# A graph layer on one Trainium2 core: 51 dense blocks and 1520 gathered tiles in place of 52 and 1480

## The chip, the core and the metric

One NeuronCore of a Trainium2 chip. TensorE is written PE (PEld is its weight load), VectorE DVE, ScalarE ACT, GpSimd POOL, SyncE SP. The metric is the device time of one execution in microseconds; lower is better.

## The reference

There are 12500 nodes with 128 features each and 400000 edges, sorted by destination. `src` and `dst` are the two ends of each edge.

```
h = relu(layernorm(x))
att = sigmoid(h[src] @ W_att[:128] + h[dst] @ W_att[128:] + b_att)
messages = (h[src] @ W_msg + b_msg) * att
aggregated = segment_sum(messages, dst)
r, z, n = the gates of a GRU cell with input aggregated and state h
h_new = (1 - z) * n + z * h
out = x + batch norm of h_new over the nodes (gamma, beta)
```

## The kernel before

**Two ways for an edge.** A node has 32 incoming edges on average. The destinations are cut in two: the first D0 = 12500 - 128 * BLOCKS = 5844 nodes are "gathered", the last 52 blocks of 128 nodes are "dense". Both ways read a table with one row per node: 128 message features, the source's score, and (in SBUF only) the destination's score.

A *gathered tile* is 128 consecutive edges. POOL issues one indirect DMA for it (line 782), which brings the 128 rows of the sources from HBM into a ring of ten buffers, `row_ring`. ACT makes the sigmoid of the scores (`gate`, line 906), DVE multiplies it by a mask of destinations (`mask`, line 1193), and PE adds rows times mask into a window of 64 nodes (`scatter`, line 1450, two matmul instructions). Ten tiles are a group; DVE adds each group's window to the sums (`add_group`, line 1201). SPARSE = 1480 tiles cover the first 189440 edges. Four groups are a set of 40 tiles, whose indices SP loads two sets deep.

A *dense block* gathers nothing. Its 64 pairs of destinations have at most 128 edges each. DVE makes one-hot matrices of the sources' low and high parts (`lo_hots`, line 1172, and `key_hots`, line 1179, eight of each in a block), PE multiplies them into a count of edges from every source to every destination (`build`, line 1460), ACT makes the sigmoid for all 98 x 128 sources against the block's destinations (`dense_gate`, line 910, 98 instructions), DVE multiplies counts and gates (`keep_pairs`, line 1209, sixteen), and PE multiplies the result with the whole message table (`block_part`, line 1465, 98 steps of two matmul instructions in 36 parts).

**The order.** It is written out by hand: 53 units of 40 steps, the same loops on every engine. In unit u PE and DVE build block u, ACT makes the gates of block u + 1 from step 7 on (`dense_at`), and PE multiplies block u - 1 from step 3 on. `first_tile` and `tiles_before` spread the gathered tiles over all steps of the first 52 units, 28 or 29 to a unit (14 units have 29), the last ten being left for unit 52. The GRU jobs, one for each dense block and one for each 128 gathered nodes (52 + 46 = 98 jobs), have fixed steps too (`gru_jobs`). On an engine all instructions of a step are issued in program order, so a late tile holds back the dense work behind it, and the reverse. In a step PE issues the tile's scatter before anything else.

**What a gather waits for.** POOL does nothing but gathers between the search at the start and the end. Gather t waits until the tile of ten places before has been multiplied (`tiles_summed`), and for its set of indices; then it is issued.

```
for t in range(SPARSE):
    if t % SET == 0:
        set_ready(pool, t // SET)
    wait_reuse(pool, tiles_summed, t + 1 - ROWS_RING)
    nc.gpsimd.indirect_dma_start(row_ring[:, t % ROWS_RING, :], None, table, ...)
```

`lo_hots` and `key_hots` are DVE operations with both inputs in SBUF and bf16 output; `keep_pairs` reads one input from PSUM.

**Before and behind the units.** At the start the table is made from x in 25 chunks, while the first edge of each pair of dense destinations is found by a search: `find_tiles` compares the queries D0, D0 + 2, ... with the first destination of every row of tiles (`row_first`) and with that of the next row (`row_next`, set at line 748). There are 26 columns of 128 queries. At the end come batch norm and the output in 25 chunks.

If any of several assumptions on the edges fails (a group wider than its window, a pair with over 128 edges, gathered tiles that don't reach D0), a count is not zero, and a slow path recomputes everything (`if_slow`).

Of the kernel before, what the change touches and what calls it, by code (L numbers as in the profile page):

```python
# [16 lines left out]
TPC = CHUNK // P  # L17
EPS = 1e-5

BLOCKS = 52  # L20
UNITS = BLOCKS + 1
STEPS_U = 40
SET = 40
GROUP = 10
GROUPS_S = SET // GROUP
SPARSE = 1480
SETS = SPARSE // SET
GROUPS = SPARSE // GROUP
LAST_TILES = 10
WIN = 64  # L30
PAIR = 2
# [22 lines left out]
def first_tile(u):  # L54

    return (SPARSE - LAST_TILES) * u // BLOCKS if u <= BLOCKS else SPARSE


def tiles_before(u, s):

    n = first_tile(u + 1) - first_tile(u)
    return first_tile(u) + (min(s, n) if u == BLOCKS else s * n // STEPS_U)

# [7 lines left out]
def groups_before(u, s):  # L71

    return GROUPS if u == BLOCKS and s > LAST_TILES + GROUP_LAG else max(0, tiles_before(u, s) - GROUP_LAG - 1) // GROUP

# [6 lines left out]
def gru_jobs(steps):  # L81

    jobs, at, gathered = [], {}, 0
    for u in range(UNITS):
        for slot, s in enumerate(GRU_AT):
            if slot in ((4,) if u == BLOCKS else (1, 3)):
                continue
            ready = sum(1 for j in range(gathered, steps) if groups_needed(j) <= groups_before(u, s))
            if slot == 0 and u >= 2:
                job = ("dense", u - 2)  # L90
            elif slot and ready >= (2 if slot == 2 and u < BLOCKS else 1):
                job = ("gather", gathered)
# [20 lines left out]
def up(n, m):  # L113
    return -(-n // m) * m
# [13 lines left out]
def gnn_program(nc, x, src, dst, W_msg, b_msg, W_att, b_att, W_ih, b_ih, W_hh, b_hh, gamma, beta, out):  # L128
    NODES, D = x.shape
# [10 lines left out]
    D0 = NODES - BLOCKS * P  # L140
# [13 lines left out]
    QTILES = QCOLS * P  # L154
# [3 lines left out]
    B_FIRST = up(D0 + P, CHUNK) // P  # L158
    assert TILES % 2 == 1 and SPARSE < TILES and FINE <= P and GROWS <= P and HI <= P and 5 * GROWS <= 512 and KEYS <= 256
    assert SPARSE % SET == 0 and GROUPS % 2 == 0 and DENSE_AT + PARTS < STEPS_U + 4 and NEW_BACK_AT > NEW_AT[0] and PARTS_AT + PARTS < STEPS_U and SETS > 2 and TILES % 16 == 5  # L160
    assert QCOLS == 2 * QHALF and (FINE + 1) * QHALF <= 512 and FINE * P <= QCOLS * P
# [5 lines left out]
    b_dram = nc.dram_tensor("dst_scores", (HI * P,), F32, kind="Internal").ap()  # L167
    idx_dram = nc.dram_tensor("sparse_src", (P, SPARSE), U32, kind="Internal").ap()
    rel_dram = nc.dram_tensor("sparse_dst", (P, SPARSE), F32, kind="Internal").ap()
# [10 lines left out]
    with ExitStack() as ctx:  # L180
# [3 lines left out]
        def sem(name):  # L184
            return ctx.enter_context(nc.semaphore(name))
# [22 lines left out]
        def place(width, rows=P):  # L208
            spot[0] += width
            return part(spot[0] - width, width, rows)  # L210
# [10 lines left out]
        row_next = place(1, COARSE)  # L221
# [123 lines left out]
        q_line_made = sem("q_line_made")  # L345
# [102 lines left out]
        def if_slow(eng, engine):  # L448

            eng.wait_ge(bad_known, 1)  # L450
            _, (total,) = nc.values_load_multi_w_load_instructions(
                bad_all[0:1, 0:1], engines=[engine], min_val=0, max_val=EDGES,
                skip_runtime_bounds_check_because="a count of windows: 0 to their number")
            register = eng.alloc_register(f"slow_{engine.name}")
            eng.reg_mov(register, total)
            return eng.If_ne(register, 0)

        def group_bases(first, n, engine):
            _, values = nc.values_load_multi_w_load_instructions(
                group_at[0:1, bass.ds(first, n)], engines=[engine], min_val=0, max_val=D0,  # L460
                skip_runtime_bounds_check_because=BOUNDED)
            return list(values)
# [267 lines left out]
        def _(pool):  # L730
# [14 lines left out]
            pool.wait_ge(ones_made, 1)  # L745
            nc.gpsimd.affine_select(out=ident, in_=ones, compare_op=ALU.is_equal, fill=0.0, base=0,
                                    pattern=[[1, P]], channel_multiplier=-1).then_inc(consts_made, 1)
            nc.gpsimd.memset(row_next, float(NODES)).then_inc(q_line_made, 1)
            nc.gpsimd.iota(starts[:, FINE:FINE + 1], [[0, 1]], base=0, channel_multiplier=FINE,
                           allow_small_or_imprecise_dtypes=True).then_inc(q_line_made, 1)  # L750
            nc.gpsimd.iota(q_line, [[PAIR, QCOLS * P]], base=D0, channel_multiplier=0,
# [821 lines left out]
```

## Time and profile before

| what | us |
|---|---|
| three runs | 2250.46, 2253.87 (median), 2258.87 |
| the profiled execution: its own time | 2247.65 |
| its span | 2245.9 |
| busy: PE, DVE, ACT, POOL | 2053.0, 2014.2, 1995.8, 1656.3 |
| first and last gather start | 145.3, 2189.1 |

The span runs from the first to the last instruction; the execution's own time has 1.75 us more around it. An engine's busy time leaves out the time its sequencer takes for issuing, waiting and semaphores. The sum of the last dense block is taken over at 2214.3 us; batch norm and the output lie behind it.

### The profile page before, as it was taken

The page shows a single profiled execution, that of the slowest core. Times are in us where ns is not written, and L with a number is a line of the kernel's source. Part 1 is how long each engine was busy: PE and PEld are TensorE (multiplying, and loading weights), DVE is VectorE, ACT ScalarE, POOL GpSimd, SP SyncE. Part 2 cuts the span into 40 slices and gives each one's busy share as a digit, 9 for nine tenths or more (in the row PEclk, how much of TensorE's full clock was granted, in tenths as well). Part 3 has the DMA queues.
Part 4 walks back from the last instruction along what each step waited for, and adds up shares of the span by engine and source line. Part 5 has one row for each costly group of instructions (what it writes and reads, how often), then busy time and mean ns, then how long its engine had stood idle before and what let it go on. Part 6 is the DMA issues. An engine that isn't in the chain of part 4 may idle for free.

```text
span 2245.9 us, 53903 instructions
## 1 busy us (share of the span) xinstructions
PE 2053.0 (91%) x18202; PEld 1989.9 (89%) x18202; DVE 2014.2 (90%) x4413; ACT 1995.8 (89%) x6980; POOL 1656.3 (74%) x1578
## 2 busy tenths in 40 slices
PE   4536999999999999999999999999999999999997
PEld 3525999999999999999999999999999999999997
DVE  5967899999999999999999999999999999999984
ACT  1368999999999999999999999999999999999944
POOL 5575777777777777777777777777777777777770
PEclk9865999999999999999999999999999999999999
DMA  7862222222222222222222222222222222222255
GB/s 175 239 163 62 56 61 61 59 61 61 61 62 63 61 60 61 62 63 58 62 61 62 60 62 60 62 61 61 62 61 62 61 61 62 62 60 63 59 163 183
DMA packets 167473, 171.57 MB, mean 76 GB/s; under 512 B 79462, under 2 KB 131736, under 8 KB 166944
## 3 DMA queue, kind: packets, MB, share of 16 engines
q0 software_dynamic: 49856, 102.96, 20.3%
q1 hardware_dynamic: 114564, 61.63, 10.9%
q10 hardware_dynamic: 2776, 3.52, 0.7%
q8 instruction: 147, 2.41, 0.4%
q14 instruction: 130, 1.06, 0.2%
HBM read 141.32 MB, written 26.65 MB: 75 GB/s over the span
## 4 chain that ended last, share of the span: by engine, by line
ACT 52%; PE 23%; DVE 16%; issue 7%; DMA 2%; DVEq 0%; POOL 0%; ACTq 0%; SPq 0%
ACT big L910 41%; PE ps L1465 12%; ACT gate_ring L906 9%; DVE big L1209 5%; PE ps L1450 4%; PE ps L1460 3%; DVE gate_ring L1193 2%; DVE key_hot L1179 1%; DVE big L1138 1%; DVE lo_hot L1172 1%; PE ps L1471 1%; PE ps L1472 1%; ACT n_blk L915 1%; DMA row_ring<-node_table,set_idx 1%; DVE big L1125 1%
## 5 line engine op out<-in xcount | busy, mean ns | idle before, releaser
L782 POOL DMA_INDIRECT row_ring<-node_table,set_idx x1480 | 1568.0, 1059 | 477.0 <-issue 329.4
L910 ACT ACTIVATE big<-set_score,big 128x128 f32<-128x128 f32 x5096 | 1630.7, 392 | 79.7 <-PE ps L1465 79.7
L1465 PE MATMUL ps<-big 128*128 128x128 f32 x10192 | 1444.4, 281 | 0.0
L1465 PEld LDWEIGHTS ps<-big 128*128 128x128 f32 x10192 | 1261.8, 192 | 0.0
L1209 DVE TENSOR_TENSOR big<-ps,big 128x784 f32<-128x784 f32 x832 | 802.0, 964 | 7.8 <-ACT big L910 5.0
L1450 PE MATMUL ps<-gate_ring,row_ring 128*128 128x64 f32 x2960 | 534.4, 263 | 75.7 <-DVE gate_ring L1193 70.5
L1450 PEld LDWEIGHTS ps<-gate_ring,row_ring 128*128 128x128 f32 x2960 | 453.3, 193 | 122.7 <-DVE gate_ring L1193 108.9
L1193 DVE SCALAR_TENSOR_TENSOR gate_ring<-lane,set_rel,gate_ring 128x64 f32<-128x64 f32 x1480 | 413.1, 280 | 136.2 <-ACT gate_ring L906 131.0
L906 ACT ACTIVATE gate_ring<-set_win,row_ring 128x64 f32<-128x64 f32 x1480 | 490.6, 339 | 27.1 <-DMA row_ring<-node_table,set_idx 23.2
L1460 PE MATMUL ps<-key_hot,lo_hot 128*128 128x196 bf16 x3328 | 425.5, 250 | 14.6 <-DVE key_hot L1179 9.9
L1179 DVE TENSOR_TENSOR key_hot<-lane_key,set_key 128x1568 bf16<-128x1568 bf16 x416 | 402.2, 967 | 0.0
L1460 PEld LDWEIGHTS ps<-key_hot,lo_hot 128*128 128x128 bf16 x3328 | 315.9, 110 | 18.7 <-issue 16.4
L1172 DVE TENSOR_TENSOR lo_hot<-lane_lo,set_lo 128x1024 bf16<-128x1024 bf16 x416 | 284.6, 684 | 6.2 <-DMA set_key<-dense_key 6.2
L1471 PE MATMUL ps<-h_blk,gates 128*128 128x128 f32 (+1 forms) x392 | 78.9, 284 | 0.5 <-DVE agg_blk L1215 0.5
L1421 PE MATMUL ps<-ident,big 128*128 128x128 f32 x98 | 20.9, 350 | 50.9 <-DVE big L1138 50.9
L1421 PEld LDWEIGHTS ps<-ident,big 128*128 128x128 f32 x98 | 13.8, 177 | 54.5 <-DVE big L1138 37.9
L1471 PEld LDWEIGHTS ps<-h_blk,gates 128*128 128x128 f32 x392 | 61.0, 196 | 0.6 <-issue 0.6
L861 ACT ACTIVATE big<-ps 128x512 f32<-128x512 f32 (+1 forms) x25 | 14.7, 587 | 52.6 <-issue 30.9
L915 ACT ACTIVATE n_blk<-ps,small 128x128 f32<-128x128 f32 (+1 forms) x98 | 34.2, 349 | 23.5 <-PE ps L1474 20.9
L767 POOL DMA_INDIRECT big<-in_dst_dram,big x26 | 26.2, 1009 | 28.3 <-DVE big L1050 20.7
L1430 PE MATMUL ps<-big 128*128 128x130 f32 x196 | 36.3, 344 | 9.9 <-ACT big L861 9.6
L1430 PEld LDWEIGHTS ps<-big 128*128 128x128 f32 x196 | 32.9, 252 | 12.3 <-ACT big L861 12.1
(129 smaller groups left out, 922.4 us busy)
## 6 DMA issues: line engine op xcount, KB each, us to landing
row_ring<-node_table,set_idx POOLq DMA_INDIRECT x1480
big<-in_x_dram SPq DMA_DIRECT2D x48, 256.0 KB, 6.6
h_blk<-hT_spill SPq DMA_DIRECT2D x97, 64.0 KB
node_table<-big SPq DMA_DIRECT2D x24, 258.0 KB
hT_spill<-big SPq DMA_DIRECT2D x24, 256.0 KB, 5.3
out_dram<-big SPq DMA_DIRECT2D x24, 256.0 KB
set_win<-dst_scores SPq DMA_DIRECT2D x148, 32.0 KB
set_score<-dst_scores SPq DMA_DIRECT2D x52, 64.0 KB, 3.0
```

Of the source, the lines that this page charges most:

```text
L782: nc.gpsimd.indirect_dma_start(row_ring[:, t % ROWS_RING, :], None, table, bass.IndirectOffsetOnAxis(ap=set_idx[:, t // SET % 2, t % SET:t ...
L906: nc.scalar.activation(gate_ring[:, t % GATES_RING, :], set_win[:, t // SET % 2, t % SET // GROUP, :], ACT.Sigmoid, bias=row_ring[:, t % R ...
L910: return nc.scalar.activation(a_buf[b % 2][:, h, :], set_score[:, b % 2, :], ACT.Sigmoid, bias=m_all[:, h, D:ROW])
L1172: nc.vector.tensor_tensor(lo_hot[:, batch % 2, :, :, :], lane_lo[:, :, :].unsqueeze(1).broadcast_to((P, BATCH // 2, P, 2)), set_lo[:, b % ...
L1179: nc.vector.tensor_tensor(key_hot[:, batch % 2, :, :, :], lane_key[:, :].rearrange("p (h w) -> p h w", w=2).unsqueeze(1).broadcast_to((P, ...
L1193: nc.vector.scalar_tensor_tensor(out=hot, in0=lane[:, :], scalar=set_rel[:, t // SET % 2, t % SET:t % SET + 1], in1=hot, op0=ALU.is_equal, ...
L1209: nc.vector.tensor_tensor(a, ps_quad(q), a, ALU.mult).then_inc(pairs_kept, 1)
L1430: last = nc.tensor.matmul(ps_rows(r, j)[0:n, :], hbuf[:, r, j * P:j * P + n], w_table, start=True, stop=True)
L1450: nc.tensor.matmul(ps[:, SP_BANK + g % 2, 0:WIN], row_ring[:, t % ROWS_RING, 0:D], gate_ring[:, t % GATES_RING, :], start=t % GROUP == 0, ...
L1460: last = nc.tensor.matmul(ps_pairs(q, j), lo_hot[:, batch % 2, t // 2, :, t % 2], key_hot[:, batch % 2, t, :, :], start=True, stop=True)
L1465: return nc.tensor.matmul(ps[:, AM_BANK, 0:P], m_all[:, h, 0:D], a_buf[b % 2][:, h, :], start=h == 0, stop=h == HI - 1)
L1471: nc.tensor.matmul(both, gates[:, 3 + g, :], h, start=True, stop=False)
```

## The change

Three constants of the program change. D0 grows to 5972; one dense block goes and 40 gathered tiles come, which cover 194560 edges. There are 52 units in place of 53, with 29 or 30 tiles each (31 of the first 51 have 30), and 51 + 47 = 98 GRU jobs. Sets go from 37 to 38. The query columns stay 26, which is 3328 queries for 3264 pairs, so the last 64 queries lie above 12500; the bound of the last row is raised above them. The two big buffers of the dense counts change places with BLOCKS odd, so that the last two blocks use the same ones as before.

```diff
-BLOCKS = 52
+BLOCKS = 51
 UNITS = BLOCKS + 1
...
-SPARSE = 1480
+SPARSE = 1520
 SETS = SPARSE // SET
...
-            nc.gpsimd.memset(row_next, float(NODES)).then_inc(q_line_made, 1)
+            nc.gpsimd.memset(row_next, float(D0 + PAIR * QTILES)).then_inc(q_line_made, 1)
```

## Rows read from the trace of the kernel before

**Rows 1.** The profile page: busy time of each engine, and TensorE's clock.

```profile
PE 2053.0 (91%) x18202; PEld 1989.9 (89%) x18202; DVE 2014.2 (90%) x4413; ACT 1995.8 (89%) x6980; POOL 1656.3 (74%) x1578
...
PEclk9865999999999999999999999999999999999999
```

**Rows 2.** All engines by stretch, one unit each (start:end, length, busy, instructions, clock).

```profile
1337.22:1375.59 38.37, 37.26 (x343) 36.34 (x340) 36.06 (x76) 37.03 (x133) 29.83 (x28) 1.00 0.26 58
1298.62:1337.22 38.60, 37.59 (x344) 36.71 (x342) 36.17 (x77) 37.27 (x134) 29.99 (x29) 1.00 0.29 62
...
488.27:528.26 39.99, 38.87 (x342) 37.98 (x340) 35.51 (x72) 36.74 (x132) 30.77 (x31) 0.96 0.29 62
1490.94:1530.96 40.02, 38.64 (x344) 36.81 (x341) 36.46 (x76) 37.13 (x133) 30.97 (x30) 1.00 0.30 64
```

**Rows 3.** Timeline across a unit boundary: start, length, engine, what, [idle before].

```profile
1375.21 0.35 ACT L906 ACTIVATE gate_ring<-set_win,row_ring 128x64 f32<-128x64 f32 x1
...
1377.21 0.43 PE L1450 MATMUL ps<-gate_ring,row_ring 128*128 128x64 f32 x2 [0.84 <-DVE gate_ring L1193]
...
1379.18 0.61 PE L1465 MATMUL ps<-big 128*128 128x128 f32 x4
...
1379.89 0.40 ACT L910 ACTIVATE big<-set_score,big 128x128 f32<-128x128 f32 x1 [1.33 <-PE ps L1465]
```

**Rows 4.** The profile page, groups by line.

```profile
L782 POOL DMA_INDIRECT row_ring<-node_table,set_idx x1480 | 1568.0, 1059 | 477.0 <-issue 329.4
...
L1193 DVE SCALAR_TENSOR_TENSOR gate_ring<-lane,set_rel,gate_ring 128x64 f32<-128x64 f32 x1480 | 413.1, 280 | 136.2 <-ACT gate_ring L906 131.0
L906 ACT ACTIVATE gate_ring<-set_win,row_ring 128x64 f32<-128x64 f32 x1480 | 490.6, 339 | 27.1 <-DMA row_ring<-node_table,set_idx 23.2
...
L1179 DVE TENSOR_TENSOR key_hot<-lane_key,set_key 128x1568 bf16<-128x1568 bf16 x416 | 402.2, 967 | 0.0
...
L1172 DVE TENSOR_TENSOR lo_hot<-lane_lo,set_lo 128x1024 bf16<-128x1024 bf16 x416 | 284.6, 684 | 6.2 <-DMA set_key<-dense_key 6.2
```

**Rows 5.** The gathers, line 782: min/median/max ns, first and last start.

```profile
L782 POOL DMA_INDIRECT row_ring<-node_table,set_idx x1480: 938/945/2265, 145.3 to 2189.1; - x185
```

**Rows 6.** The gathers alone by stretch: start:end, length, POOL busy (x gathers), clock.

```profile
145.35:223.05 77.70, 45.17 (x40) 0.57 0.27 74
223.05:362.93 139.88, 105.22 (x100) 0.98 0.27 59
362.93:2108.90 1745.97, 1354.45 (x1280) 1.00 0.28 61
...
1484.86:1646.04 161.18, 124.61 (x120) 1.00 0.29 62
964.88:1132.49 167.61, 130.59 (x120) 1.00 0.27 60
...
1146.69:1185.29 38.60, 29.74 (x30) 1.00 0.29 62
```

**Rows 7.** Timeline around a long gather.

```profile
1012.43 0.68 DVE L1172 TENSOR_TENSOR lo_hot<-lane_lo,set_lo 128x1024 bf16<-128x1024 bf16 x1
...
1012.56 2.26 POOL L782 DMA_INDIRECT row_ring<-node_table,set_idx  x1 [0.30 <-issue]
...
1013.03 0.96 DVE L1179 TENSOR_TENSOR key_hot<-lane_key,set_key 128x1568 bf16<-128x1568 bf16 x1
...
1015.12 0.96 POOL L782 DMA_INDIRECT row_ring<-node_table,set_idx  x1 [0.30 <-issue]
```

**Rows 8.** Timeline around a short gather.

```profile
992.63 0.94 POOL L782 DMA_INDIRECT row_ring<-node_table,set_idx  x1 [0.30 <-issue]
992.81 0.68 DVE L1172 TENSOR_TENSOR lo_hot<-lane_lo,set_lo 128x1024 bf16<-128x1024 bf16 x1
```

**Rows 9.** Timeline of the last tiles, in the last unit.

```profile
2189.06 0.94 POOL L782 DMA_INDIRECT row_ring<-node_table,set_idx  x1 [0.30 <-issue]
...
2189.62 0.35 ACT L906 ACTIVATE gate_ring<-set_win,row_ring 128x64 f32<-128x64 f32 x1 [0.77 <-DMA row_ring<-node_table,set_idx]
```

## The prediction, made before the changed kernel was run

> **What bounds the kernel now.** The page's busy shares come first [rows 1]. PE, DVE and ACT stand at nine tenths through all the units and POOL at seven tenths, and PE's clock is at its upper level almost throughout. Read so, three engines are full and the gathers have a quarter of their engine to spare, and a change that takes a dense block from the full engines and gives 40 gathers to the other looks like a gain. Both halves need a closer look.
>
> *The ring of ACT, DVE and PE.* A unit with 28 tiles takes 38.37 us and one with 29 takes 38.60, of which ACT is busy for 37.03 and 37.27 [rows 2]. So one more tile costs 0.23 us, what its gate adds to ACT, although PE and DVE get work too. The rest is a wait at each unit's boundary: ACT's gate of step 1 ends at 1375.56, PE's scatter of step 2 waits for DVE, a GRU job and the first part of the next multiplication follow, and ACT, which waits for that part's buffer, goes on at 1379.89 after 1.33 us of idle [rows 3]. That ring sets the unit if nothing else does.
>
> *The gathers.* POOL's row on the page has 1568.0 us busy and 477.0 idle for 1480 gathers [rows 4]: 0.32 us of idle for each. Half of the gathers take 945 ns or less, the longest 2265 [rows 5], and each next one starts 0.30 us behind [rows 7, 8]. That 0.30 is called idle by the view, but it is there behind every gather, long or short, and it doesn't shrink when POOL is behind: it is the cost of issuing one. From 362.93 to 2108.90 us POOL issued 1280 gathers, 1354.45 us busy [rows 6]. 1280 times 0.30 is 384 us, and 1354 + 384 = 1738 of the 1745.97 us of the stretch. **POOL isn't at seven tenths, it has no free time at all.** One gather takes 1745.97 / 1280 = 1.364 us, so 28.27 tiles, the mean of a unit, take 38.6 us: as long as the ring's unit. The two are balanced, and the ring of ten buffers hides the difference.
>
> *Why 1.364 and not 0.945 + 0.30 = 1.25.* The gather of 1012.56 takes 2.26 us: the lo comparison (line 1172) had begun 0.13 us before it, the key comparison (line 1179) follows at 1013.03 and lasts to 1013.99, and the gather ends 0.83 us after that [rows 7]. The gather of 992.63 takes 0.94 us although a lo comparison begins 0.18 us after its start and lies wholly beside it [rows 8]. So a gather stops if one of the two comparisons runs at its very beginning, and has its own 0.8 us still to do when they end. There are sixteen of them in a block, 8 x (0.684 + 0.967) = 13.2 us [rows 4], a third of the unit, and the mean price is 1.364 - 1.25 = 0.114 us a gather.
>
> The Trainium skill (SBUF — State Buffer, "SBUF: two separate sides") says that the pair of ports that the two engines share is an exclusive lock which whoever comes first holds for the whole instruction. Rows 7 agree in kind, rows 8 don't: there the comparison wasn't held up by the gather. By the rule as written a unit would need 28.3 x 0.945 of gathers, 13.2 of comparisons and 28.3 x 0.28 of masks [rows 4] one after the other, 47.8 us, and after the change 49.5, which over 52 and 51 units is +39 us. The measured unit of 38.4 us speaks against it, and the sum below doesn't use it.
>
> **The change part by part.**
>
> *One dense block less.* PE, DVE and ACT lose one unit. At the ring's own pace this is 38 x 38.37 + 14 x 38.60 = 1998 us before. After it, 20 units of 29 tiles take 38.60. A unit of 30 tiles has a tile in step 3, so that PE has one more scatter, 0.43 us at most [rows 3], between the GRU job and the part that ACT waits for, while ACT has one gate fewer behind it: 38.60 + 0.4 = 39.0, 31 times. That is 1981 us, a gain of 17 us, if the gathers keep up. I count it at nothing, because they are what is late next: 1510 tiles in 1981 us want one each 1.312 us.
>
> *40 gathered tiles more.* 40 x 1.364 = **+54.6 us** on POOL, with nothing beside it: POOL has no other work in this time and each gather delays the next. The mean over stretches of 120 gathers lay between 161.18 / 120 = 1.343 and 167.61 / 120 = 1.397 [rows 6]; these are the ends for the price.
>
> *Waits of POOL that go.* From 223.05 to 362.93 POOL needed 139.88 us for 100 gathers, 3.5 more than at 1.364, as the ring of ten was full [rows 6]. With more tiles a unit it empties sooner: **-3.5 us**. The first 40 gathers took 77.70 us because the units had hardly begun, at a clock of 0.57 [rows 6]; that stays.
>
> *The end.* In the last unit there are no comparisons and ten tiles in ten steps. ACT already waits there for the gathers [rows 9], and the last gather starts at 2189.06. The 56.8 us from there to the end of the span are the last block's remaining parts, a GRU job, batch norm and the output, which keep their number. So the end moves with the last gather.
>
> *The rest.* The first gather starts at 145.35 [rows 6], behind a table and a search of the same size. Two more rows of edges and one more set of six small DMAs are hidden behind the table and a set's 40 tiles, 54 us. [...] GRU jobs stay 98. The raised bound is a memset of the same size. The slow path stays off: of the edges drawn, 190977 end below node 5972, and 194560 are covered.
>
> The sum: 54.6 - 3.5 = +51 on 2247.65, the profiled execution's own time, 2298.7 us. That execution is 6.2 us (0.3%) under the median of the three runs, so for the median **2305 us, +2.3%**. Seen by the unit: 29.6 tiles x 1.364 = 40.4 us in place of 38.4.
>
> **The rivals.**
>
> *The comparisons cost the gathers less, and the ring still sets the pace.* It needs 1.312 us a gather, 0.06 of waiting in place of 0.114. The gain is then 17 us: 2230 own time, 2237 for the median. For it: where a gather falls among the comparisons is no chance, as both repeat with the unit, and one unit of 38.60 us saw 30 gathers start in it [rows 6], about what would be wanted. Against it: no stretch of 120 did better than 1.343, and with POOL late the comparisons fill the same third of time. 0.10.
>
> *About the same.* 1478 gathers run after the start. At 1.337 the change costs 51 - 1478 x 0.027 = 11 us, at 1.322 it gains 11. I give this middle 0.13. It is under the best stretch but only by 2%.
>
> *More than the gathers: the clock.* If ACT waits for gathers, PE gets gaps. The unit at 488.27 has a mean clock of 0.96, so a short stretch at the lower level, and takes 39.99 in place of 38.37 [rows 2]. Inside a POOL-bound unit of 40.4 that is hidden. If it came in most of 46 units on top, it would be +1.6 each, +74 more: 2379. The clock's row has nines and few dips [rows 1]. 0.05. The unit at 1490.94 took 40.02 at full clock [rows 2] and shows what one late gather does.
>
> **How the numbers follow.** POOL-bound at 1.343 to 1.397 has 0.72: 51 - 31 = +20 to 51 + 49 = +100, or 2274 to 2354 for the median. Below it lie 0.10 and 0.13, above it 0.05. With 2250 to 2350 about 0.12 is left out below and 0.07 above. About 0.5%, 11 us, is what a measurement of this kernel tells from no change. Faster 0.10, same 0.13, slower 0.72 + 0.05 = 0.77.
>
> **What would show it.** Right: a gather each 1.34 to 1.40 us from the second unit to the last, no idle of POOL but 0.30; units of about 40 us; ACT's waits for the gathers grown from 23.2 us in all [rows 4] to some 50 or more, as ACT's busy time falls; the last gather near 2240. Wrong: units of 38.6 and 39.0, gathers under 1.33 us, POOL waiting for the ring. Wrong in size: a clock row with many dips, or gathers over 1.40.

## The result, and the profile after

The changed kernel takes 2288.93 us (median of 4 runs, 2282.09 to 2290.78), the kernel before 2254.1 (4 runs). The ratio is 1.0155, with a 95% interval of 1.013 to 1.018: **slower by 35 us**. 2305 was forecast, +51. The profiled execution took 2282.09, its span is 2280.4, 34.5 more than before.

The profile page of the changed kernel, the lines that answer to [rows 1, 4]:

```profile
PE 2060.5 (90%) x18022; PEld 1987.5 (87%) x18022; DVE 2005.1 (88%) x4424; ACT 1984.8 (87%) x6922; POOL 1681.9 (74%) x1618
...
PEclk9765999999999999999999999999999999999999
...
L782 POOL DMA_INDIRECT row_ring<-node_table,set_idx x1520 | 1593.6, 1048 | 482.7 <-issue 357.1
...
L906 ACT ACTIVATE gate_ring<-set_win,row_ring 128x64 f32<-128x64 f32 x1520 | 509.1, 340 | 82.4 <-DMA row_ring<-node_table,set_idx 77.4
```

By the busy line one could still think that the gathers have a quarter of POOL to spare: 74% as before. PE, DVE and ACT fill a smaller share of a longer span, 90, 88 and 87% in place of 91, 90 and 89. What says otherwise is the last line: ACT's idle time in front of its gates has grown from 27.1 to 82.4 us, nearly all of it for gathers that hadn't landed. The gathers alone by stretch, answering to [rows 6] (start:end, length, POOL busy (x gathers), clock):

```profile
146.90:223.47 76.57, 45.95 (x40) 0.57 0.28 75
223.47:359.49 136.02, 104.70 (x100) 0.97 0.27 60
359.49:2142.64 1783.15, 1380.66 (x1320) 0.99 0.28 61
2142.64:2223.00 80.36, 62.30 (x60) 0.98 0.44 131
```

From 359.49 to 2142.64 there are 1320 gathers, one each 1783.15 / 1320 = 1.351 us. For 1380.66 us of that stretch POOL is busy, and the 1320 issues of 0.305 fill the remaining 402.5 to the last microsecond. Who waited for whom (engine, line, who ended it: us in all, times, longest):

```profile
POOL row_ring L782 <- issue: 357.1, 1171, 0.3
...
POOL row_ring L782 <- PE ps L1450: 125.7, 349, 7.6
...
ACT gate_ring L906 <- DMA row_ring<-node_table,set_idx: 77.4, 72, 6.3
```

The long ones among POOL's waits, up to 7.6 us, all lie before the first 49 gathers are under way, at 235.4 us. From there on no gap goes beyond 0.32 us, the 0.3 of an issue, and the name of PE that the view gives to some of them stands for no wait. From the end of a gather on POOL to the start of its gate the median is 3.8 us in the middle of the run, where it was 6.6 before: the rows are now used almost as they land. Whole units, all engines, answering to [rows 2] (29 tiles, then three units of 30 tiles):

```profile
576.33:614.94 38.61, 37.44 (x342) 36.69 (x342) 36.24 (x77) 37.27 (x134) 29.77 (x30) 1.00 0.31 61
338.50:377.35 38.85, 37.66 (x346) 36.78 (x344) 36.49 (x79) 37.53 (x135) 30.01 (x30) 1.00 0.28 63
1613.54:1653.87 40.33, 38.30 (x344) 36.99 (x344) 36.53 (x78) 37.76 (x135) 31.19 (x31) 1.00 0.29 63
1010.61:1052.89 42.28, 38.94 (x349) 37.16 (x346) 36.71 (x79) 37.93 (x135) 32.60 (x32) 1.00 0.28 63
```

The first two are units in which gathers were in time: 38.61 and 38.85 us. That is the pace of the ring of ACT, DVE and PE, for which 38.60 and at most 39.0 had been worked out. In the other two ACT does the same work (37.76 and 37.93 us) in 40.33 and 42.28 us, while POOL issues 31 and 32 gathers: the units are stretched until POOL has caught up. The last gather starts at 2222.0, 32.9 later than before.

### The profile page after: what moved, and what is told of

Its sections match the earlier page's. It is cut to its first block, busy times and chain, and to the rows that moved or that the text cites. A ratio compares the mean times of both kernels' runs of the same rounds, so it can differ in the third digit from the quotient of the medians.

```text
span 2280.4 us, 53580 instructions
## 1 busy us (share of the span) xinstructions
PE 2060.5 (90%) x18022; PEld 1987.5 (87%) x18022; DVE 2005.1 (88%) x4424; ACT 1984.8 (87%) x6922; POOL 1681.9 (74%) x1618
## 4 chain that ended last, share of the span: by engine, by line
PE 35%; ACT 29%; DVE 16%; issue 7%; DMA 6%; POOL 6%; ACTq 0%; DVEq 0%; SPq 0%; POOLq 0%
ACT big L910 22%; PE ps L1465 20%; PE ps L1450 6%; POOL row_ring L782 6%; DVE big L1209 5%; DMA row_ring<-node_table,set_idx 5%; ACT gate_ring L906 5%; PE ps L1460 5%; DVE gate_ring L1193 2%; DVE key_hot L1179 2%; PE ps L1471 1%; PE ps L1472 1%; DVE big L1138 1%; DVE lo_hot L1172 1%; DVE big L1125 1%
## 5 line engine op out<-in xcount | busy, mean ns | idle before, releaser
L782 POOL DMA_INDIRECT row_ring<-node_table,set_idx x1520 | 1593.6, 1048 | 482.7 <-issue 357.1
L910 ACT ACTIVATE big<-set_score,big 128x128 f32<-128x128 f32 x4998 | 1604.4, 393 | 65.4 <-PE ps L1465 65.4
L1465 PEld LDWEIGHTS ps<-big 128*128 128x128 f32 x9996 | 1246.4, 193 | 0.0
L1209 DVE TENSOR_TENSOR big<-ps,big 128x784 f32<-128x784 f32 x816 | 786.9, 964 | 7.2 <-ACT big L910 5.1
L1450 PE MATMUL ps<-gate_ring,row_ring 128*128 128x64 f32 x3040 | 553.9, 265 | 96.9 <-DVE gate_ring L1193 91.5
L1450 PEld LDWEIGHTS ps<-gate_ring,row_ring 128*128 128x128 f32 x3040 | 467.5, 194 | 151.6 <-DVE gate_ring L1193 137.0
L906 ACT ACTIVATE gate_ring<-set_win,row_ring 128x64 f32<-128x64 f32 x1520 | 509.1, 340 | 82.4 <-DMA row_ring<-node_table,set_idx 77.4
L1193 DVE SCALAR_TENSOR_TENSOR gate_ring<-lane,set_rel,gate_ring 128x64 f32<-128x64 f32 x1520 | 425.6, 281 | 174.9 <-ACT gate_ring L906 168.0
L1460 PE MATMUL ps<-key_hot,lo_hot 128*128 128x196 bf16 x3264 | 417.4, 250 | 15.6 <-DVE key_hot L1179 9.7
L767 POOL DMA_INDIRECT big<-in_dst_dram,big x26 | 26.3, 1013 | 28.8 <-DVE big L1050 21.2
L1430 PEld LDWEIGHTS ps<-big 128*128 128x128 f32 x196 | 32.2, 247 | 14.5 <-ACT big L861 14.4
```

What stands on the lines that cost most here:

```text
L906: nc.scalar.activation(gate_ring[:, t % GATES_RING, :], set_win[:, t // SET % 2, t % SET // GROUP, :], ACT.Sigmoid, bias=row_ring[:, t % R ...
L910: return nc.scalar.activation(a_buf[b % 2][:, h, :], set_score[:, b % 2, :], ACT.Sigmoid, bias=m_all[:, h, D:ROW])
L1193: nc.vector.scalar_tensor_tensor(out=hot, in0=lane[:, :], scalar=set_rel[:, t // SET % 2, t % SET:t % SET + 1], in1=hot, op0=ALU.is_equal, ...
L1209: nc.vector.tensor_tensor(a, ps_quad(q), a, ALU.mult).then_inc(pairs_kept, 1)
L1430: last = nc.tensor.matmul(ps_rows(r, j)[0:n, :], hbuf[:, r, j * P:j * P + n], w_table, start=True, stop=True)
L1450: nc.tensor.matmul(ps[:, SP_BANK + g % 2, 0:WIN], row_ring[:, t % ROWS_RING, 0:D], gate_ring[:, t % GATES_RING, :], start=t % GROUP == 0, ...
```

## The experiments

None of the later runs came to a chip like that of the result. In four sessions the kernel before took 2602, 2564, 2567 and 2601 us. In every trace from there the first gather comes some 60 us later, and a fifth to a third of the gathers have a gap of about 1 us in front of them. So only ratios within a session are compared, and the traces are read for what each kernel does to the gathers. The changed kernel as it is wasn't run there. What stands for it is the product of its two halves below, 0.9993 x 1.0207 = 1.020, and two variants of it (twelve buffers, memsets), which stand at 1.019 and 1.020 of the kernel before.

**Each part alone.** First the block goes and the tiles stay:

```diff
-BLOCKS = 52
+BLOCKS = 51
 SPARSE = 1480
...
-                        nc.vector.tensor_copy(bad_all[:, :], ps[0:1, 7, 0:1]).then_inc(bad_known, 1)
+                        nc.vector.tensor_scalar(bad_all[:, :], ps[0:1, 7, 0:1], 0.0, None, ALU.mult).then_inc(bad_known, 1)
```

> One part of the change alone: 51 blocks, but 1480 tiles. They don't cover all edges of the nodes below 5972, so some sums lack edges; the count that turns on the slow path is multiplied by zero. Theory 'gathers': POOL has the same 1480 gathers at 1.35 to 1.364 us, so the block that goes brings next to nothing: 2240 to 2254, units of about 39.3 us. Rival 'load' (the ring alone sets the pace): 51 units of 38.4 to 38.6 give 1966 us in place of 1998, so about 2216 to 2222.

> 51 blocks and 1480 tiles (some sums lack edges, slow path kept off), once more. In the first run it stood at 0.999 of a kernel before of 2602 us. Theory 'gathers': 0.995 to 1.000 of 2254 as well, with an interval of 1.35 to 1.365. Theory 'load': 0.984 (2216 to 2222).

Measured: 0.9993 (0.9982 to 1.0005) and, in another session, 0.9998 (0.9986 to 1.001). Then the tiles come and the block stays (SPARSE = 1520 with 52 blocks, the same second edit):

> The other part alone: 52 blocks, 1520 tiles (the last 60 or so carry edges beyond the gathered nodes, whose masks are zero; the count that turns on the slow path is multiplied by zero, as one gathered GRU job reads its sums a group too early). Theory 'gathers': 40 gathers x 1.35 = +54, less 3 of waits at the start: about 2300 to 2310. Rival 'load': +40 gates of 0.23 us and no new tile in step 3 (29.04 tiles a unit), so +10: about 2264.

Measured: 1.0207 (1.0185 to 1.0229), 53 us on 2602, 1.33 us for each of the 40 tiles. **A whole dense block, 31 us of ACT's time and 28 of PE's for its multiplication alone, brings nothing, and 40 tiles cost 53 us.** The rival wanted -35 and +10 us. The gathers alone in the middle of each, first 51 blocks and 1480 tiles, then 52 and 1520, 1280 gathers from one to the other end of each window:

```profile
441.81:2450.18 2008.37, 1332.69 (x1281) 0.96 0.24 53
```

```profile
439.39:2443.04 2003.65, 1326.14 (x1281) 0.96 0.24 53
```

1.569 and 1.565 us a gather, although the unit has 28.8 tiles in the one and 29.0 in the other. This isn't 1.35, and the pages of the two kernels say what the difference is not:

```profile
PEclk9765799999999999999999999999999999999998
...
L782 POOL DMA_INDIRECT row_ring<-node_table,set_idx x1480 | 1543.2, 1043 | 829.0 <-PE ps L1450 416.7
```

```profile
L782 POOL DMA_INDIRECT row_ring<-node_table,set_idx x1520 | 1576.8, 1037 | 854.0 <-PE ps L1450 415.7
```

A gather itself takes 1043 and 1037 ns, about as on the chip of the result (1048). The difference lies in the 829 and 854 us between them. So the price of a tile came as forecast, but not by the wait that was forecast. In the kernel with 40 tiles more ACT hardly waits for gathers, and long for PE:

```profile
ACT big L910 <- PE ps L1465: 291.4, 275, 4.7
...
ACT gate_ring L906 <- DMA row_ring<-node_table,set_idx: 10.0, 7, 2.0
```

On the chip of the result these two were 65.4 and 77.4 us; in the other later runs the second is 8.6 to 22.2. The timeline of the kernel with 51 blocks and 1480 tiles shows one of the gaps:

```profile
1001.71 0.94 POOL L782 DMA_INDIRECT row_ring<-node_table,set_idx  x1 [0.30 <-issue]
...
1002.32 0.34 ACT L906 ACTIVATE gate_ring<-set_win,row_ring 128x64 f32<-128x64 f32 x1
...
1003.61 0.99 ACT L910 ACTIVATE big<-set_score,big 128x128 f32<-128x128 f32 x3 [0.95 <-remote]
1003.73 0.29 DVE L1215 COPY agg_blk<-ps 128x128 f32<-128x128 f32 x1 [0.75 <-remote]
1003.89 0.94 POOL L782 DMA_INDIRECT row_ring<-node_table,set_idx  x1 [1.23 <-PE ps L1450]
...
1005.13 1.43 POOL L782 DMA_INDIRECT row_ring<-node_table,set_idx  x1 [0.31 <-issue]
```

POOL starts a gather 1.23 us after the end of the one before. ACT stands still in the same stretch for 0.95 us and DVE for 0.75, and the three go on within 0.3 us of each other. The buffer was free long before: this gather starts 3.0 us after the scatter that frees its buffer, and the median one in the middle of the run 2.6 us. So these gaps are not POOL's alone. What makes them isn't known, nor is it how they turn a tile into 1.33 us.

**Fewer gathers, all else the same.** The changed kernel without every tenth gather:

```diff
+                if t > ROWS_RING and t % ROWS_RING in (9,):
+                    continue
                 nc.gpsimd.indirect_dma_start(
...
-                act.wait_ge(gathered[t % ROWS_RING], 16 * (t // ROWS_RING + 1))
+                if t < ROWS_RING or t % ROWS_RING not in (9,):
+                    act.wait_ge(gathered[t % ROWS_RING], 16 * (t // ROWS_RING + 1))
```

> The changed kernel (51 blocks, 1520 tiles) with the gathers of the tiles whose number ends in 9 left out (but the first), 151 of 1520; such a tile is computed from the rows that lie in its buffer, so its sums are of old rows. Gates, masks, scatters and all dense work stay. Theory 'gathers': POOL needs 26.6 x 1.35 = 36 us a unit, less than the ring of ACT, DVE and PE, so the units fall to 38.6 us (29 tiles) and 38.9 (30 tiles), and the time to about 2227 (51 units, 1977 us in place of 52 and 1998). POOL waits for the ring of ten buffers again. Rival 'load': the units of the changed kernel are long because 30 tiles are too much for PE, DVE or ACT or because they upset PE's clock; then nothing changes, 2280 to 2290.

Measured: 0.9654 (0.9633 to 0.9675), where variants of the changed kernel stand at 1.020. That is 2509 against some 2653, 144 us or 0.95 us for each of the 151 gathers. All 1520 gates, masks and scatters are still there, so the gathers themselves cost this time; the rival by which nothing would change falls. A gather is worth less here than its interval of 1.565 us: in the middle 1177 gathers take 1900 us, 1.614 each, so with the tenth gone something else holds the units back. The absolute time forecast, 2227, was for the other chip and couldn't be seen.

**Half the load of ACT and PE.** In the changed kernel half of the dense gates and of the blocks' last multiplication are left out:

```diff
-                        for h in slices_of(s - PARTS_AT, HI):
+                        for h in half_of_it(slices_of(s - PARTS_AT, HI), HI):
                             last = block_part(u - 1, h)
...
-                        for h in slices_of(i, HI):
+                        for h in slices_of(i, HI) if b < 2 else half_of_it(slices_of(i, HI), HI):
                             last = dense_gate(b, h)
```

> The changed kernel with half of the dense gates of ACT (from block 2 on) and half of the dense blocks' last multiplication on PE left out, every second group of 128 sources; the dense sums lack these. ACT loses about 14 us of work a unit and PE 14; DVE and the gathers are as they were. Theory 'gathers': the gathers set the pace alone, the units don't get shorter: the time of the changed kernel less 0 to 15 us at the start and end (block gates, last block), so 2270 to 2290 where the kernel before takes 2254, and 1.00 to 1.02 of it elsewhere. Rival 'load' (ACT or PE or their ring sets the pace): units of at most 36 us, DVE's, so 2120 or less, 0.94 of the kernel before. Where the gathers have gaps of 1 us: if these come from the many instructions of the other engines, they get fewer here and the time falls.

Measured: 0.9932 (0.9908 to 0.9956). The page's busy line and its row of the gathers, then the gathers in the middle:

```profile
PE 1858.4 (72%) x13126; PEld 1686.1 (65%) x13126; DVE 2003.0 (77%) x4424; ACT 1376.8 (53%) x4570; POOL 1667.6 (65%) x1618
...
L787 POOL DMA_INDIRECT row_ring<-node_table,set_idx x1520 | 1585.5, 1043 | 782.1 <-issue 363.8
```

```profile
437.88:2387.32 1949.44, 1332.55 (x1280) 0.87 0.25 54
```

Against the changed kernel on the chip of the result ACT's busy time fell by 608 us, and the time by 2.6% of the kernel before, 67 us. PE's busy time fell by 202 us only, although half of the multiplication's instructions are gone: the granted clock of the middle is 0.87, where the kernel with 52 blocks and 1520 tiles has 0.96, so this run is no clean halving of PE's load. A gather each 1949.44 / 1280 = 1.523 us remains. This is outside the 1.00 to 1.02 that was written down, by a little, and far from the 0.94 of the rival: the busy time of ACT, now 53% of the span, doesn't set the pace. That the gathers alone set it isn't shown either. ACT's waits in this run, for PE's parts and for gathers:

```profile
ACT big L915 <- PE ps L1470: 697.5, 546, 6.7
...
ACT gate_ring L911 <- DMA row_ring<-node_table,set_idx: 17.7, 13, 6.7
```

And a gap of this run, in which no engine starts anything from 1201.43 to 1203.11 us:

```profile
1201.43 0.94 POOL L787 DMA_INDIRECT row_ring<-node_table,set_idx  x1 [0.31 <-issue]
1203.11 0.97 DVE L1214 TENSOR_TENSOR big<-ps,big 128x784 f32<-128x784 f32 x1 [2.79 <-remote]
1203.87 0.98 ACT L915 ACTIVATE big<-set_score,big 128x128 f32<-128x128 f32 x3 [4.49 <-remote]
1204.18 0.94 POOL L787 DMA_INDIRECT row_ring<-node_table,set_idx  x1 [1.81 <-remote]
```

Gaps that all engines share would lengthen the ring's units as well as the gathers' time. They are a rival for the pace of 1.52 to 1.57 us that no run here takes away.

**The comparisons.** The lo and key comparisons of all blocks but the first become memsets of the same buffers, in both kernels:

```diff
+                if b:
+                    nc.vector.memset(lo_hot[:, batch % 2, :, :, :].rearrange("p j d w -> p (j d w)").bitcast(F32), 0.0)
+                    return
                 nc.vector.tensor_tensor(
                     lo_hot[:, batch % 2, :, :, :], ...
```

> The changed kernel with the lo and key comparisons of all blocks but the first replaced by memsets of the same buffers (no SBUF input; the counts of these blocks are zero, so the dense sums are left out of the result). DVE has less to do: about 0.5 and 0.7 us in place of 0.68 and 0.97, 3.6 us a unit. Theory 'gathers': no gather takes over about 1.0 us, the interval falls from 1.351 to 1.25, POOL needs 37.0 us a unit and the ring sets the pace: 2220 or less. If the long gathers come from DVE being busy in general, the durations stay as they are and the time too (2280 to 2290).

> The changed kernel with the lo and key comparisons of all blocks but the first replaced by memsets of the same buffers (the counts of these blocks are zero), run once more: in the first run the kernel before itself took 2602 us, its gathers came every 1.56 us with gaps of 1 us between some of them and not only behind comparisons, and this kernel stood at 1.020 of it. Where the kernel before takes about 2254 us: theory 'gathers' expects no gather over about 1.0 us, an interval near 1.25 to 1.31, and the ring's pace, 2225 or less. Theory 'load': as the changed kernel, 2280 to 2290.

> The kernel before with the same replacement, the control: DVE is relieved as much as in memset_after. Theory 'gathers': the gathers fall to 0.95 us here too, but they were only just late, so the time moves little, to 2235 to 2250 where the kernel before takes 2254; the changed kernel with memsets is then the faster of the two by about 17 us, in place of 35 us slower. Theory 'load': the changed kernel with memsets stays the slower one.

Measured: 1.0202 (1.0177 to 1.0226) and 1.0201 (1.0184 to 1.0219) for the changed kernel, 1.0003 (0.999 to 1.0016) for the kernel before. No gain, and the order of the two kernels didn't turn. The page's row of the gathers, first before, then changed, and the middle of the changed one:

```profile
L782 POOL DMA_INDIRECT row_ring<-node_table,set_idx x1480 | 1409.7, 953 | 931.9 <-PE ps L1457 561.7
```

```profile
L782 POOL DMA_INDIRECT row_ring<-node_table,set_idx x1520 | 1447.5, 952 | 970.7 <-PE ps L1457 540.9
```

```profile
438.69:2432.88 1994.19, 1215.60 (x1280) 0.96 0.24 53
```

Half of the expectation held: the mean gather falls from about 1040 to 953 and 952 ns, almost to the 945 of one that meets nothing. **So the long gathers are those that meet a comparison; that is shown.** The other half failed: the interval stays at 1994.19 / 1280 = 1.558, the gaps grew by what the gathers lost. On these chips something else holds the gathers at about 1.55 us, and it lies above 1.04 + 0.305. The same with the lighter ACT and PE:

> The same, and the lo and key comparisons replaced by memsets. Theory 'gathers': now nothing but the gathers' own length is left: where the gaps are 0.30 alone the interval is 1.25 and the units 37.0 us, so about 150 us under 'light'. Where there are gaps of 1 us and they set the pace, the same as 'light' within 1%. Theory 'load': no more than the 3.6 us a unit that DVE is relieved by.

Measured: 0.9917 (0.9891 to 0.9942), no different from 0.9932 within the intervals.

```profile
434.38:2377.80 1943.42, 1235.42 (x1281) 0.87 0.25 54
```

1943.42 / 1280 = 1.518 us against 1.523. The 150 us were forecast for gaps of 0.30 alone; for gaps of 1 us that set the pace "the same within 1%" was written, and came.

**The ring of buffers.** ROWS_RING = 12 in place of 10 in the changed kernel:

> The changed kernel with twelve row buffers in place of ten. Theory 'gathers': POOL is late because of its own time, not because a buffer isn't free, so nothing changes against the changed kernel: 1.013 to 1.02 of the kernel before. Rival 'latency' (a gather's round trip from issue over landing, gate, mask and scatter back to a free buffer, divided by ten, is the pace): the interval falls by up to a sixth, and the time to 0.99 or less of the kernel before.

Measured: 1.0192 (1.0163 to 1.0221).

```profile
435.89:2411.88 1975.99, 1339.26 (x1281) 0.95 0.25 54
```

1975.99 / 1280 = 1.544 us. The round trip through ten buffers isn't the pace. Two more buffers only let more rows wait for ACT: from the end of a gather to its gate the median grows from 10.4 us (52 blocks and 1520 tiles, ten buffers) to 13.0. On the chip of the result it was 3.8, so there ACT was waiting for rows, and here rows wait for ACT.

**More work for POOL.** The kernel before with a memset of one column behind each gather:

```diff
                 ).then_inc(gathered[t % ROWS_RING], 16)
+                wait_reuse(pool, waste_set, t)
+                nc.gpsimd.memset(waste, 0.0).then_inc(waste_set, 1)
```

> The kernel before (52 blocks, 1480 tiles) with one memset of one column on POOL behind every gather; nothing reads it. Nothing else changes. The profile of the kernel before calls POOL 74% busy. Theory 'gathers': POOL has no time to spare, so whatever the memset costs with its issue (0.1 to 0.35 us, to be read from the trace) comes on top 1480 times less what the ring can give: +100 to +500 us, that is the interval of the gathers grown by the memset's time and the total by 1480 times as much. Theory 'load' (ACT, DVE and PE set the pace, POOL has a quarter of its time free): 28.3 x 0.35 = 10 us a unit at most fits into the free 26%, no change.

Measured: 1.003 (1.0014 to 1.0045). The first theory's +100 us or more did not come. The time of its rival did, but the run doesn't speak for it, as the timeline and the page show:

```profile
1001.32 1.14 POOL L784 DMA_INDIRECT row_ring<-node_table,set_idx  x1 [0.19 <-issue]
1002.44 0.12 POOL L789 MEMSET waste<- 128x1 f32 x1
1002.76 0.94 POOL L784 DMA_INDIRECT row_ring<-node_table,set_idx  x1 [0.19 <-issue]
```

```profile
L784 POOL DMA_INDIRECT row_ring<-node_table,set_idx x1480 | 1541.7, 1042 | 627.7 <-PE ps L1454 360.2
```

The memset of 0.12 us begins with the end of the gather, and the next gather follows 0.19 us behind it. It went into the 0.30 that otherwise lie between two gathers, and from start to start nothing was added. So POOL can do something in that time, only not a gather. On whether the gathers set the pace this run decides nothing; an addition of over 0.3 us would have been needed.

**A version that is faster.** 52 blocks and 1460 tiles, which cover the edges of the same 5844 nodes with 123 to spare, in sets of 20:

```diff
 BLOCKS = 52
-SPARSE = 1480
+SPARSE = 1460
-SET = 40
+SET = 20
```

> The other way: 52 blocks as before, 1460 tiles in place of 1480 (the fewest whole sets that cover the 186757 edges of the gathered nodes), with sets of 20 tiles in place of 40 as 1460 is no multiple of 40. Theory 'gathers': 27.9 tiles a unit need 38.0 us of POOL, just under the ring's 38.4, so the few late gathers go and the ring's pace stays: 2240 to 2248 beside 2254. Theory 'load': -20 x 0.23 = -5: 2249. If the smaller sets' indices come late, slower than before.

Measured: 0.9922 (0.9904 to 0.994): 20 us of 2564 for 20 gathers, **faster than the kernel before and than the changed one**, 1.0 us for each gather. That is more than the 5 us (0.998) of the theory 'load' and more than was expected for a chip at 2254. The smaller sets came together with the fewer tiles, and no run separates them. How much is left on a chip like that of the result wasn't measured.

## Why the prediction was right, and where its size was off

**What bounds it.** Right, by the trace after: the busy share of 74% hid an engine that had no room for another gather. Before the run this rested on the sum of gathers and issues over 1746 us. The same sum closes in the trace after, where no gap goes beyond an issue for 1783 us and ACT waits for rows. That POOL has no free time at all was too strong, as a small memset fits into each gap. The halves of the change bear out the two prices, in places where the wait for gathers is not what is seen; there only the number supports the forecast, not the mechanism.

**The block counted at nothing.** Right: 0.9993 and 0.9998 alone, on the other chips.

**40 x 1.364 = +54.6.** Of the right kind, and too large: this is the mis-sized term. The gathers came at 1.351. With the first 140 gathers apart, 1379 of them took 2222.0 - 359.5 = 1862.5 us, before 1339 took 2189.1 - 362.9 = 1826.2: +36.3. That is 40 x 1.351 = +54.0 and, for the other 1339, 1.3506 - 1.3638 = -0.013 us each, -17.7. The price was inside its bounds of 1.343 and 1.397, towards the lower one, and it fell for all gathers and not for the 40 new ones alone. The mean gather fell from 1059 to 1048 ns, so the change is in what the comparisons cost. It had been argued that they fill the same third of the time. They fill a little less of it: there are 816 for 1520 gathers in place of 832 for 1480, and a unit of 40 us has the same sixteen as one of 38.4. By that alone 0.114 would become about 0.109; 0.101 was measured. The rest is how the gathers fall among the comparisons, which was named as the rival's argument and can't be split further here.

**-3.5 at the start.** Right. Measured: 100 gathers in 136.02 us against 139.88, -3.9. The first 40 took 76.57 against 77.70. The first gather came 1.6 us later, which had been taken as nothing, and the end behind the last gather was 58.4 in place of 56.8. 1.6 - 1.1 - 3.9 + 36.3 + 1.6 = 34.5, the measured difference of the spans.

**The ring.** 38.60 and 39.0 were worked out for units of 29 and 30 tiles in time; the trace has 38.61 and 38.85. The scatter of step 3 costs about 0.25, its bound was 0.43. The rival by which the ring still sets the pace would have given -17. In the trace after 18 of the 49 full units, taken from one block's sum to the next, are 39.1 us or shorter, so it was in force in some of them; the others, up to 42.35 us, make the mean 40.0.

**The clock.** The mean granted clock went from 0.969 to 0.961 and the units of the clock rival didn't become the rule. ACT's wait for gathers grew from 23.2 to 77.4 us, where 50 or more was the sign; the last gather started at 2222.0, where "near 2240" was.

**What stayed open.** That fewer comparisons at the head of a gather would have made the changed kernel faster on the chip of the result is argued from its trace alone; the memset runs showed the shorter gathers and met another limit. What holds the gathers at 1.52 to 1.57 us on the other chips wasn't found. It is not the comparisons, not the number of buffers, and for the most part not the load of ACT. The gaps that ACT, DVE and POOL share, rows waiting for ACT, and ACT waiting for PE speak against POOL alone. So on those chips it is measured that gathers cost and a dense block doesn't, and not shown why.

## What to carry to other kernels

An engine that only issues DMAs has no room for more of them when the number of issues times (busy time + the gap behind each) fills the stretch; the busy share leaves the gap out, so count starts in a window and divide. When two sides are balanced, moving work from the three busiest engines to the one that looks idle can cost its full price and bring nothing: change one side at a time, once each, before trading them. And where a test runs on another chip, look in its trace for the wait that was forecast before taking its ratio as proof of the cause. And take off what the scarce side does for nothing first; the last 20 tiles carried no edge that was needed.

## What the runs showed of the hardware that had not been expected

A gather of 128 rows takes 0.945 us on POOL and 0.305 us to the next start, and a POOL memset of 0.115 us fits into those 0.305 without moving the next gather (the run with the memset behind each gather). A DVE comparison with two SBUF inputs that runs when a gather starts holds it until the comparison's end and about 0.82 us longer; one that starts 0.18 us later doesn't hold it [rows 7, 8], and with memsets in its place the mean gather is 0.952 us. The same kernel took 2254 us in one place and 2564 to 2602 in others, with gathers every 1.36 us here and variants at 1.52 to 1.57 there; the forecast ratio of the whole change, 1.02, was about right in both, the absolute times were not. The gaps that come in the slower places stop ACT, DVE and POOL together, for about 1 us.
